# A four-stage network on one core: the first batch's rows in four places, the weights' rounding moved, and parts of q and k written four times in another order

## What is computed

```python
x = x + attention0(layernorm(x))   # one head, keys and values of 64, causal over 2048 rows
x = x + ffn0(layernorm(x))         # clip(x).astype(fp8) @ clip(weight).astype(fp8).T + bias
x = x + attention1(layernorm(x))   # 16 heads of 16, rotary positions, causal
x = x + ffn1(layernorm(x))         # mixes each row with the one before; r * (relu(k)**2 @ W_v.T)
```

## Time and profile before

| | us |
|---|---|
| three runs | 2739.13, 2739.94, 2746.29; median 2739.94 |
| the profiled execution, in all | 2741.72 |
| its span, first to last instruction | 2739.8 |
| PE busy | 2477.3 (90%) |
| DVE busy | 1998.2 (73%) |
| ACT busy | 1555.1 (57%) |
| POOL busy | 596.8 (22%) |
| mean granted clock of PE | 0.964 |

### The profile page before, as it was taken

One profiled execution on the slowest core, in us unless ns is written; L12 is line 12 of the kernel. 1 busy time (PEld: TensorE's weight loads), 2 busy tenths in 40 slices (PEclk: granted clock), 3 DMA queues, 4 the chain that ended last, 5 costly groups with the idle time before them and its releaser, 6 DMA issues.

```text
span 2739.8 us, 57369 instructions
## 1 busy us (share of the span) xinstructions
PE 2477.3 (90%) x21618; PEld 1129.0 (41%) x21618; DVE 1998.2 (73%) x4256; ACT 1555.1 (57%) x2785; POOL 596.8 (22%) x584
## 2 busy tenths in 40 slices
PE   5788789999999999999989999899999989999996
PEld 3444233433444444343434434343344433433344
DVE  4666688787877687768876687877777769888822
ACT  2234456576655556556655556556565656666662
POOL 4544120303114121221303313031222310000011
PEclk8899899999999999999999999999999999999998
DMA  1433222121311313030221312213031131111110
GB/s 44 115 99 102 86 76 59 48 86 41 98 40 44 109 46 101 25 110 25 70 72 42 96 53 81 61 46 104 17 108 38 36 110 54 40 50 42 30 39 28
DMA packets 238911, 176.09 MB, mean 64 GB/s; under 512 B 88752, under 2 KB 238384, under 8 KB 238640
## 3 DMA queue, kind: packets, MB, share of 16 engines
q1 hardware_dynamic: 237872, 171.51, 21.9%
q10 hardware_dynamic: 768, 0.92, 0.1%
HBM read 87.36 MB, written 84.41 MB: 63 GB/s over the span
## 4 chain that ended last, share of the span: by engine, by line
PE 57%; DVE 21%; SPq 7%; ACT 6%; issue 4%; DMA 3%; POOL 1%; DVEq 1%; POOLq 0%; ACTq 0%
PE psum L1721 13%; DVE mx L1421 13%; PE psum L1698 11%; PE psum L1669 6%; SPq L852 4%; PE psum L1637 4%; ACT probs L1196 3%; PE psum L1601 2%; PE psum L1572 2%; PE psum L1511 2%; PE psum L1752 2%; PE psum L1741 2%; PE psum L1772 2%; PE psum L1656 2%; PE psum L1760 2%
## 5 line engine op out<-in xcount | busy, mean ns | idle before, releaser
L1196 ACT ACTIVATE probs<-psum 128x512 f32<-128x512 f32 x2176 | 1143.8, 604 | 627.8 <-PE psum L1698 398.2
L1421 DVE TENSOR_REDUCE mx<-psum 128x1 f32<-128x512 f32 (+2 forms) x2304 | 1289.3, 622 | 260.8 <-PE psum L1669 167.5
L1698 PE MATMUL psum<-qst,kst 34*128 34x512 bf16 (+7 forms) x5120 | 667.6, 352 | 51.8 <-ACT probs L1196 15.5
L1721 PE MATMUL psum<-probs,vs 128*17 128x512 f32 (+3 forms) x5120 | 595.5, 547 | 1.8 <-ACT probs L1196 0.9
L1669 PE MATMUL psum<-kst,qst 64*128 64x512 bf16 (+3 forms) x2560 | 438.8, 356 | 88.1 <-DMA qst<-rest_dram 29.3
L1698 PEld LDWEIGHTS psum<-qst,kst 64*128 64x128 bf16 (+1 forms) x5120 | 195.1, 95 | 395.0 <-DVE mx L1421 122.7
L1669 PEld LDWEIGHTS psum<-kst,qst 64*128 64x128 bf16 x2560 | 133.0, 94 | 415.6 <-ACT probs L1196 149.9
L1721 PEld LDWEIGHTS psum<-probs,vs 128*17 128x17 f32 x5120 | 93.3, 96 | 195.9 <-issue 162.5
L990 POOL TENSOR_SCALAR vare<-mv 128x4 f32<-128x4 f32 x64 | 15.3, 238 | 657.1 <-DVE mv L1298 657.1
L1146 ACT ACTIVATE probs<-psum 128x1024 f32<-128x1024 f32 x80 | 74.9, 940 | 109.5 <-PE psum L1586 54.1
L1676 PE MATMUL psum<-maskq,identh 64*128 64x64 bf16 (+1 forms) x2048 | 128.6, 206 | 0.0
(11 more groups left out here) (160 smaller groups left out, 2848.8 us busy)
## 6 DMA issues: line engine op xcount, KB each, us to landing
main_dram<-parts SPq DMA_DIRECT2D x224, 128.0 KB
qst<-main_dram SPq DMA_DIRECT2D x128, 128.0 KB, 2.7
kst<-main_dram SPq DMA_DIRECT2D x128, 128.0 KB, 2.8
rest_dram<-parts SPq DMA_DIRECT2D x112, 128.0 KB
v_dram<-vst SPq DMA_DIRECT2D x64, 136.0 KB, 3.9
vs<-v_dram SPq DMA_DIRECT2D x64, 136.0 KB, 2.2
xs<-x_in SPq DMA_DIRECT2D x16, 512.0 KB, 4.0
x_dram<-xs SPq DMA_DIRECT2D x16, 512.0 KB, 3.0
```

Of the source, the lines that this page charges most:

```text
L1196: act.activation(dst, src, ACT.Exp, scale=DK1 ** -0.5).then_inc(S["exp"], 1)
L1421: ins = dve.tensor_reduce(mx1[:, n % 2, 2 * g + odd, tile % TPC, c:c + 1], bank(src, at, at + cols), AX.X, ALU.max)
L1698: ins = pe.matmul(two[odd][:, at:at + cols], kst[rows, kslot, part, pair, keys], qst[rows, qslot, part, pair, CH - cols:CH], start=(part = ...
L1721: ins = pe.matmul(bank(7, off, CH, rows=VW, row=32 * h), vtile[:, h, :], probs[:, HG * (step_no(b, hg, k) % 2) + h, at:at + CH - off], sta ...
```

## The change

- Each chunk of the first batch has its own place for rows of x: two in `xs`, one in `attc`, one in `x3T` (buffers of the last stage). Rows of batch 0 are all loaded at the start; later batches use the two places of `xs` as before. `seat`, `seat_before` and `seat_uses` say which place, who had it, and how often it was filled; `rows_before` and `columns_readers` give the waits for xn and xnT, since chunks 2 and 3 are now normalised before chunks 0 and 1 have gone on.
- At the start SP issues the loads of the ffn0 weights and of all four chunks ahead of the two DMAs of wo0. The rounding is a job of its own, "wf8", after norm 0 of chunk (0, 0), and waits only for its weights; their bias has a semaphore of its own.
- `bias0` must come after "turnmax0 d" of (0, 0) in the planner. POOL's masks are made behind the first root instead of the second.
- A put writes four rows of parts for each head, STORED: (0, 1, 2, 0) for q and (0, 1, 0, 2) for k, in one tensor `qk_dram`. A load is six DMAs of 32 rows: for even and for odd heads one of rows 0 and 1, one more of rows 0 and 1 (q) or 1 and 2 (k), and one of the last two. The products are the same six.
- Blocks are counted half first: 0 is q and 1 is k of heads 0 to 7, then 2 and 3 of heads 8 to 15. Before, 0 and 1 were q, 2 and 3 k.
- PATIENCE is 0.25 instead of 0.2, and the planner's latency of a put 5.0 instead of 6.0.

```diff
-TERMS = [(0, 0), (0, 1), (1, 0), (1, 1), (0, 2), (2, 0)]
-MAIN = 4
-REST = (len(TERMS) - MAIN) * DK1
+
+STORED = ((0, 1, 2, 0), (0, 1, 0, 2))
+PAIRED = ((0, 0), (0, 1))
...
+def seat(b, q):
+
+    return q if b == 0 else q % 2
+
+
+def seat_before(b, q):
+
+    if b == 0:
+        return None
+    if q >= 2:
+        return (b, q - 2)
+    return (b - 1, q + 2 if b > 1 else q)
+
+
+def seat_uses(b, q):
+
+    return 1 if b == 0 else 2 * b + q // 2
+
+
+def rows_before(ln, b, q):
+
+
+    if b == 0 and ln < 2:
+        if q < 2:
+            return (0, b, q + 2) if ln else None
+        return (2, b, q - 2) if ln else (0, b, q - 2)
+    if ln:
+        return (ln - 1, b, q)
+    return (2, *shared(b, q)) if shared(b, q) else None
+
+
+def columns_readers(ln, b, q):
+
+    last = shared(b, q)
+    first = None
+    if b == 0 and q < 2:
+        first, last = ((b, q + 2) if ln else None), None
+    elif b == 0:
+        first, last = ((b, q - 2), None) if ln == 0 else (None, last)
+    elif ln:
+        first, last = (b, q), None
+    jobs = [("QK0", first), ("V0", first)] if first else []
+    return jobs + ([("QK1", (*last, t)) for t in range(TPC)] + [("V1", (*last, n)) for n in range(2)] if last else [])
 
 
 def block_no(b, hg, q):
...
-PATIENCE = 0.2
+PATIENCE = 0.25
...
-    add("SP", "load x", c, key() - (60.0 if b else 1e4), 0.1, ("store x2", p2), ("norm", p2 and (2, *p2)), lat=4.0)
+    add("SP", "load x", c, key() - (60.0 if b else 1e4), 0.1, ("store x2", seated), ("norm", seated and (2, *seated)),
+        lat=4.0 if b else (4.0, 9.0, 12.0, 15.0)[q])
     norm(0, ("load x", c))
-    turn(0, *[("QK1", same and (*same, t)) for t in range(TPC)], *[("V1", same and (*same, n)) for n in range(2)])
+    turn(0, *columns_readers(0, *c))
     last = same and ("scores0", (*same, TPC * (same[1] + 1) // 2 - 1))
-    add("POOL", "bias0", c, key(0), 2.4, ("norm", (0, *c)))
+    add("POOL", "bias0", c, key(0), 2.4, ("norm", (0, *c)), ("turnmax0 d", (0, 0)))
+    if c == (0, 0):
+        add("DVE", "wf8", c, key(), 6.5, ("norm", (0, *c)))
     add("PE", "QK0", c, key(), 1.71, *both(0), lat=0.1, claim="P", mode="F")
...
-        add("SP", "put", (*c, bl), key(0.3), 0.6, ("lo", (*c, bl)), lat=6.0)
+        add("SP", "put", (*c, bl), key(0.3), 0.6, ("lo", (*c, bl)), lat=5.0)
...
+        seats = (xs[:, 0, :, :], xs[:, 1, :, :], attc[:, :, :],
+                 x3T[:, :, :].rearrange("p c n -> p (c n)")[:, 0:TPC * D].rearrange("p (t d) -> p t d", t=TPC))
+
+        def rows_of(b, q):
+            return seats[seat(b, q)]
+
...
             load_x(0, 0)
             for dst, src in [
                 (wqk0[:, :, :], cw(w["wqk0"])), (bqk0[0:DK0, :], w["bqk0"]), (bqk0[DK0:P, :], w["bqk0"]),
                 (wv0[:, :, :], cw(w["wv0"])),
-                (wo0[0:DK0, 0:D], w["wo0"]), (wo0[DK0:P, 0:D], w["wo0"]),
             ]:
                 sp.dma_start(dst, src).then_inc(S["weights"], 16)
             sp.dma_start(raw, cw(w["wf"])).then_inc(S["weights f"], 16)
             load_x(0, 1)
+            load_x(0, 2)
+            load_x(0, 3)
+            for rows in (slice(0, DK0), slice(DK0, P)):
+                sp.dma_start(wo0[rows, 0:D], w["wo0"]).then_inc(S["weights"], 16)
             sp.dma_start(bf[:, :], w["bf"].rearrange("(a d) -> a d", a=1).broadcast_to([P, D])
-                         ).then_inc(S["weights f"], 16)
+                         ).then_inc(S["weights b"], 16)
 
             for kind, item in ORDER["SP"]:
                 if kind == "load x":
                     b, q = item
...
-                    side, half = divmod(bl, 2)
+                    half, side = divmod(bl, 2)
                     wt.job("lo", item)
-                    for n, term in enumerate(TERMS):
-                        to, at = (main_dram, n) if n < MAIN else (rest_dram, n - MAIN)
-                        rows = to[b, side, 8 * half:8 * (half + 1), at, :, CH * q:CH * (q + 1)]
-                        sp.dma_start(rows, split(b, bl)[:, term[side], :]).then_inc(S[f"put {bl}"], 16)
+                    for n, part in enumerate(STORED[side]):
+                        rows = qk_dram[b, side, 8 * half:8 * (half + 1), n, :, CH * q:CH * (q + 1)]
...
-                        sp.dma_start(into[HALF * odd:HALF * (odd + 1), slot, 0, :, :],
-                                     main_dram[b, side, heads, :, :, cols].rearrange("g n d t -> (n d) g t")
-                                     ).then_inc(loaded, 16)
-                        sp.dma_start(into[HALF * odd:HALF * odd + REST, slot, 1, :, :],
-                                     rest_dram[b, side, heads, :, :, cols].rearrange("g n d t -> (n d) g t")
-                                     ).then_inc(loaded, 16)
+                        of = qk_dram[b, side, heads, :, :, cols].rearrange("g n d t -> n d g t")
+                        for part, row, first in [(0, 0, PAIRED[side][0]), (0, REST, PAIRED[side][1]), (1, 0, 2)]:
+                            row += HALF * odd
+                            sp.dma_start(into[row:row + REST, slot, part, :, :],
+                                         of[first:first + 2, :, :, :].rearrange("n d g t -> (n d) g t")
+                                         ).then_inc(loaded, 16)
...
-                    if item == (0, 0, 1):
+                    if item == (0, 0, 0):
                         masks(n)
-                    elif item != (0, 0, 0) and pieces < KRING:
+                    elif pieces < KRING:
                         pool.memset(kst[:, pieces, 1, :, :], 1.0).then_inc(done, 1)
...
+                        wt.job("turn", rows_before(ln, b, q))
...
+                elif kind == "wf8":
+                    eight_bit_weights()
...
-                        eight_bit_weights()
...
-                    wt.wait_ge("ready", 2)
+                    wt.job("wf8", (0, 0))
...
+                    half, side = divmod(bl, 2)
+                    cols = slice(D * side + P * half, D * side + P * (half + 1))
                     for t in range(TPC):
-                        ins = pe.transpose(ps[:, P * t:P * (t + 1)], ropeds[lane(b, q)][:, t, P * bl:P * (bl + 1)], ident[:, :])
+                        ins = pe.transpose(ps[:, P * t:P * (t + 1)], ropeds[lane(b, q)][:, t, cols], ident[:, :])
```

More of the change, by code:

```diff
@@ L324, in chunk_jobs @@
     c = (b, q)
-    p, p2, same = before(b, q), before(b, q, 2), shared(b, q)
+    p, same, seated = before(b, q), shared(b, q), seat_before(b, q)
     add = o.add
@@ L330, in norm @@
         add("POOL", "root", (ln, *c), key(), 1.33, ("stats", (ln, *c)), ("norm", same and (ln, *same)))
-        old = (2, *same) if ln == 0 and same else (ln - 1, *c) if ln else None
         add("DVE", "norm", (ln, *c), key(), 1.3, ("root", (ln, *c)),
-            ("turn", old))
+            ("turn", rows_before(ln, *c)))
     def turn(ln, *after):
@@ L392, in chunk_jobs @@
     add("POOL", "bias", c, key(), 2.4, ("norm", (1, *c)))
-    add("PE", "FFN", c, key(), 0.9, *both(1), lat=0.1, claim="D", mode="F")
+    add("PE", "FFN", c, key(), 0.9, *both(1), ("wf8", (0, 0)), lat=0.1, claim="D", mode="F")
     add("ACT", "ffn", c, key(), 0.93, ("FFN", c), *[("addf", p and (*p, n)) for n in range(2)], free=("FFN", c))
@@ L398, in chunk_jobs @@
     add("SP", "store x2", c, key(), 0.1, ("addf", (*c, 0)), ("addf", (*c, 1)), lat=3.0)
[L399 removed]
+    turn(2, *columns_readers(2, *c))
     for t in range(TPC):
@@ L524, in tail_jobs @@
     add("POOL", "carry", c, key(), 0.2, *[("mix", p and (*p, i)) for i in range(2)],
-        *[("prod", p and (*p, i)) for i in range(2)])
+        *[("prod", p and (*p, i)) for i in range(2)],
+        *([("store x2", (0, 3)), ("norm", (2, 0, 3))] if c == (0, 0) else []))
     turn(3, ("norm", (3, *c)), ("carry", c))
@@ L818, in _ @@
                     b, q = item
-                    old = before(b, q, 2)
+                    old = seat_before(b, q)
                     if old:
@@ L1101, in _ @@
                         continue
-                    if ln == 0:
-                        for t in range(TPC):
-                            wt.job("QK1", old and (*old, t))
-                        for n in range(2):
-                            wt.job("V1", old and (*old, n))
-                        dst = xnTs[at][:, :, :]
-                    elif ln == 2:
-                        wt.job("QK0", (b, q))
-                        wt.job("V0", (b, q))
+                    if ln in (0, 2):
+                        for reader in columns_readers(ln, b, q):
+                            wt.job(*reader)
                         dst = xnTs[at][:, :, :]
@@ L1312, in _ @@
                     else:
-                        src, dst = xs[:, q % 2, :, :], xns[lane(b, q)]
-                        earlier = (ln - 1, b, q) if ln else old and (2, *old)
-                        wt.job("turn", earlier)
+                        src, dst = rows_of(b, q), xns[lane(b, q)]
+                        wt.job("turn", rows_before(ln, b, q))
                     for t in range(TPC):
```

56 lines of the change are left out of this document (31 added, 25 removed).

## The result

The changed kernel takes 2670.36 us (median of four runs, 2667.99 to 2679.32) against 2740.4 (2739.13 to 2746.29): ratio 0.9746, interval 0.972 to 0.9773.

A forecast was written before the change was run, and what follows sets the result against it. PE bounds 400 to 2640 us; in the first 400 the order of the first batch's chain decides. Terms -26 - 5 + 3 = -28, and 1.8 off for plain runs, from 2741.7: 2712 us, range 2685 to 2743.

The forecast's parts named there:

- The first batch, -31 forecast: First 400 us: -26 us up to the first scores of chunk 3, -5 for chunks 2 and 3 behind that.
- The start: Start of batch 0: earlier first normalisation and moved rounding bring the first scores 9 us earlier, 5 at worst.
- up to 4.6: Normalisations of chunks 2 and 3 on DVE beside POOL's bias adds: up to 4.6 us, counted only in the worst case.
- the 34 of the forecast: Start of batch 0: first scores stand near 34 us instead of 43.25.
- the fillers: PE's 15 extra jobs for chunks 2 and 3, 18.5 us, taken to fill lost time, keeping chunk 0's lead at 10.
- Scores of chunk 3, forecast 154: First batch: first put at 91.5, 76 DMAs at 0.76 us (57.8), so these scores near 154 instead of 181.0.
- The rounding, 5.5 forecast: Rounding of 8-bit weights on DVE, in its new place: 5.5 us instead of 9.6, starting at 12.9.
- the row of 0.41 us: A rounding step on DVE taking 0.41 us beside a POOL add, read as evidence against the skill's blocking rule.
- The rest of the program, +3 forecast: After the first batch: SP has 77 us more to do, later loads cost +3 us, ends -20 and +30.
- (4): Rival, after 400 us: longer loads on SP delay PE at up to 48 blocks, +31 to 2771 us; chance 0.15.
- (1): Rival, more gain: second stretch gains 20 instead of 5, later waits mostly go (-10), 2684 us; chance 0.17.
- SP itself is mostly waiting for work, which speaks against it: After 400 us: argument that SP's queue has slack, set against the rival of longer loads.

The follow-up runs named there:

- e1: Kernel before with PATIENCE 0.25 alone, changing only the order of jobs: 2746.61 us, ratio 1.002.
- e3: Kernel before with blocks counted half first alone, old storage: 2729.67 us, ratio 0.9969.
- e6: Kernel before, old storage and six writes a put, each load's 64-row DMA split into two of 32 rows, six DMAs a load: 2746.27 us, 1.0037.
- e7: e2 with two DMAs of 16 KB, read by nothing, added to each put: 2720.94 us, ratio 0.993.
- e2: Kernel before with the new storage alone (four writes a put, six DMAs a load), same lists of jobs: 2696.46 us, ratio 0.9843.
- e5: e2 with four DMAs a load instead of six, the same six products: 2687.55 us, ratio 0.982.
- e4: Changed kernel with old storage, block count, PATIENCE and put latency, leaving four places for rows, rounding, masks and start loads: 2716.35 us, ratio 0.9912.
- e11: Kernel before, planner counting a put at 3.4 us instead of 0.6 and a load at 2.4 instead of 0.4: 2707.68 us, ratio 0.9884.
- e9: Changed kernel with POOL's first-stage bias adds in batch 0 only behind the normalisation of chunk 3: 2665.64 us, ratio 0.9736.
- b3: Changed kernel with four DMAs a load, e9's edit and a semaphore of its own for wo0: 2656.54 us, ratio 0.9698.
- e10: e4 with the rounding of the weights behind the first transposed maxima again: 2725.36 us, ratio 0.9945.
- e12: Changed kernel, planner counting a put at 2.3 us and a load at 3.6: 2642.67 us, ratio 0.964.

## Why the prediction was wrong, step by step

How far each kernel is ahead of the one before can be read at the division that ends a head group, on DVE. The first column is head group 1 of chunk 0 in batch 0 (438.67 us before), the second the last of all (2683.65), the third what is gained between them. The fourth is the share of that gain that shows as less busy time of PE between the two marks, for nearly the same instructions (2101.2 us before, 2084.7 in the changed kernel); the rest is idle time. The last adds PE's and ACT's waits for landings of puts and loads after 400 us. Each row is one profiled execution; those of e1 and e3 are 8 and 11 us below their medians.

| | ahead, 438.67 | ahead, 2683.65 | between | of it less PE busy | waits |
|---|---|---|---|---|---|
| before | 0 | 0 | 0 | 0 | 43.2 |
| e6, six writes, six loads | 2.9 | -2.9 | -5.8 | -0.6 | 50.7 |
| e7, tiny DMAs | 6.7 | 25.0 | 18.3 | 6.8 | 27.4 |
| e2, new storage | 17.2 | 46.8 | 29.6 | 10.6 | 18.0 |
| e5, and loads of four | 21.4 | 58.3 | 36.9 | 14.8 | 13.8 |
| e4, places and start | 25.7 | 22.7 | -3.0 | -0.6 | 49.4 |
| e1, PATIENCE | -7.2 | 3.6 | 10.9 | 11.1 | 52.2 |
| e3, half first | 12.0 | 24.5 | 12.4 | 8.0 | 43.4 |
| e11, costs on before | 18.5 | 35.6 | 17.1 | 8.6 | 10.3 |
| changed kernel | 28.0 | 73.8 | 45.8 | 16.5 | 12.2 |

- **The first batch, -31 forecast: 28 measured, in part by luck.** Its path was another. The start was to give 9 and gave nothing. The blocked normalisation took 6.6 us more than alone; I had it as "up to 4.6" for two and left it out of the value taken. The shared semaphore of wo0 no step named. Both are shown: e9 brings the first scores 5.2 us forward, to 38.60, and b3 another 3.9, to 34.69, the 34 of the forecast. From the first scores to the first put it took 58.2 us before and 61.0, 60.9 and 61.1 in the changed kernel, e9 and b3. So 3 us were lost where I had the fillers free; that it was the fillers is likely, and no run took them out. Hence the put at 104.83, not 91.5. Nor do the parts add up here: the storage alone is 17.2 us ahead at the first mark, the half-first count 12.0, the places 25.7, all together 28.0. I had no gain of the storage's own in this part but a shorter queue.
- **Scores of chunk 3, forecast 154: 159.2.** The queue in between was overpriced, 58 us forecast for 76 DMAs; from the first put to the rows of maxima it took 51.9, or 0.68 each. With a hand-over that was shorter too (2.5 us from the issue of these rows to the scores), this made up for 8 of the 13 us of the late start. e4 alone is 26 us ahead at 438 us and 23 at the end: nothing of this part grows later.
- **The rounding, 5.5 forecast: 6.1** (13.78 to 19.93). It began 0.9 us late, since chunk 1's rows were there at 12.04 and not at 11.1. Its new place is worth some 9 us at the end (e4 against e10). What it no longer meets is the adds: in e10 four steps took 2.5 us each.
- **Port lock.** By the row of 0.41 us I weakened the Trainium skill's rule (SBUF - State Buffer, "SBUF: two separate sides": the later one of DVE in a two-port mode and GpSimd is blocked for the whole instruction). The 7.96 us normalisation, the four steps of e10 and the 1.36 us of e9 agree with it. Nor did the fast steps speak against it, as I had them do: by that rule the one that starts first has the ports, and that can be DVE.
- **The rest of the program, +3 forecast: the step that failed.** Between the two marks the changed kernel gains 45.8 us. The new storage alone is worth -43 at the end, of which 17 lie in the first batch and 26 to 30 behind. Three things were wrong in the step. First, I counted SP's time as +77 us. Added up over the traces' issues it is 236.5 to 150.8 us for the puts and 320.7 to 357.8 for the loads: 49 less. The term of the loads was mis-sized, +154 at 0.60 us an issue, where they took 37 more, since a DMA of half the rows issues in 0.43. Second, I let small DMAs land no sooner (2.5); they land in 2.0. Third, I looked only at PE's own waits for q rows, not at ACT's for the places of parts, which each put holds from its first write to its last landing. From e6 to e5 the waits listed fall by 36.9 us, and the gain "between" rises by 42.7.
- **Waits are not all of it.** Of those 42.7 us, 15.4 are less busy time of PE at a higher granted clock (0.98 and 0.99 between the marks), and 27.3 less idle time. So the two sums do not show that a us of wait is worth a us. e1 and e3 gain 11 and 12 us between the marks with no less waiting, most of it as busy time. The clock also moves by itself: of twelve executions of the kernel before, those at 0.971 took 2730.8 and 2732.2 us, those at 0.964 to 0.966 2735.8 to 2741.6. Whether it rises because PE waits less was not tested.
- **Why a queue that mostly waits costs anything.** The planner counts 0.6 us for a put and 0.4 for a load, so it places the splitting and the scores before their transfers are done. With costs near the traced ones the kernel before gains 32 us and the waits fall from 43 to 10. I take this for the mechanism behind the storage's gain too, since fewer DMAs are fewer us that the lists had not allowed for; that is argued, not shown. The two gains add: e12 takes 28 off the changed kernel. How much of e11's gain is waits and how much another order isn't settled: 33 us of waits go behind 400 us, but it gains only 17 there, half of it as busy time, and 18 in the first batch.
- **Rivals.** (4), longer loads, has the right price in e6 (+7, 5.8 of it behind the first batch), far from 31: PE waits for q rows as often as before, five times. (1) had the waits going, -10, and 20 instead of 5 in the second stretch, and reached 2684; it came nearest, still 14 us above what was measured.
- **"SP itself is mostly waiting for work, which speaks against it".** This argument against (4) hid the gain also. SP issues for 788 of 2740 us, but at a chunk's puts it is solid for 8 us, twice (1193.47 to 1201.14 is one such place), and others wait.

## What to carry to other kernels

A queue with little to do still sets the time where its jobs come in bursts: look at the longest solid stretch and at who waits for its last landing, on every engine, ACT too. Where a planner writes the lists, set its costs beside the traced issue times of each job before anything else is tuned: 32 us came here from the costs of two kinds of job. Add up a queue's time from traced issues of the shape in question: half the rows took 0.43 us and not 0.60, and that was most of the way from +77 to -49. A semaphore that counts several loads is as late as the last of them, so a load that moves back takes the others' readers along.
